# A fused two-layer attention and expert kernel on one core: zeros on TensorE first, value weights and first context tiles in halves

## The reference

```python
x = x + xattn0(layernorm(x), ctx, ctx)      # 64 heads of 8 channels, linear attention:
#   qh = softmax(q over a head's 8 channels); kh = softmax(k over the 512 channels of a row)
#   kvs = kh^T v per head;  out = qh kvs
x = x + ffn0(layernorm(x), U1, V1, U2, V2, b1, b2)
x = x + xattn1(layernorm(x), ctx, Wq, Wk, Wv, Wo)   # k, v = [ctx, layernorm(x)] @ Wk.T, Wv.T
x = x + experts(layernorm(x), ...)                  # top 4 of 16 experts, and a shared one
```

## Time and profile before

| what | value |
|---|---|
| median of 3 runs | 724.55 us (724.33 to 725.87) |
| the profiled execution's own time | 721.26 us |
| its span, first to last instruction | 719.2 us |
| PE busy | 681.9 us, 95% of the span |
| DVE / ACT / POOL busy | 47% / 28% / 24% |
| mean granted PE clock | 0.99 |

### The profile page before, as it was taken

The page is one execution under the profiler, slowest core; times in us unless marked ns, Lnnn a source line. Parts: engine busy times, 40 slices in busy tenths (PEclk is TensorE's granted clock), DMA queues, the critical chain, the costliest instruction groups (busy, mean ns, idle before and its releaser), DMA issues.

```text
span 719.2 us, 9656 instructions
## 1 busy us (share of the span) xinstructions
PE 681.9 (95%) x2428; PEld 392.0 (55%) x2429; DVE 341.2 (47%) x831; ACT 200.6 (28%) x562; POOL 175.9 (24%) x226
## 2 busy tenths in 40 slices
PE   5999999999999999999999999999898999999991
PEld 3555344446777777767776665544343444444440
DVE  3898332532223546576675767555132333223330
ACT  4453332323335433333323342231111111111110
POOL 2344310101000000040404324264032322232332
PEclk9999999999999999999999999999999999999997
DMA  9999996004000020010104102028878757866544
GB/s 328 410 420 420 422 422 284 0 6 170 1 0 1 1 88 0 1 59 1 59 1 147 58 1 118 1 88 190 300 180 193 180 102 179 216 140 105 93 61 56
DMA packets 54481, 98.97 MB, mean 138 GB/s; under 512 B 6528, under 2 KB 27776, under 8 KB 53792
## 3 DMA queue, kind: packets, MB, share of 16 engines
q1 hardware_dynamic: 24704, 69.02, 26.0%
q0 software_dynamic: 8816, 18.00, 12.6%
q10 hardware_dynamic: 20928, 11.54, 5.6%
HBM read 44.50 MB, written 54.17 MB: 137 GB/s over the span
## 4 chain that ended last, share of the span: by engine, by line
PE 78%; DMA 10%; DVE 4%; issue 2%; ACT 1%; SPq 1%; ACTq 1%; POOL 1%; POOLq 1%; DVEq 0%
PE ps L1110 44%; PE ps L1271 11%; DMA out<-rq,sidx 8%; PE ps L1240 4%; PE ps L1101 4%; PE ps L1256 4%; PE ps L1189 3%; PE ps L1190 3%; PE ps L1199 2%; DVE rq L910 2%; DMA rq<-in_Wv 1%; PE ps L1209 1%; DMA kv<-in_experts 1%; PE ps L1133 1%; PE ps L1134 1%
## 5 line engine op out<-in xcount | busy, mean ns | idle before, releaser
L1110 PE MATMUL ps<-kv,rq 128*128 x432 | 194.8, 599 | 4.8 <-SPq L482 3.7
L1110 PEld LDWEIGHTS ps<-kv,rq 128*128 128x128 f32 x432 | 79.4, 191 | 93.7 <-issue 93.2
L1110 PE MATMUL ps<-zT,r 128*128 128x256 f32 (+1 forms) x424 | 103.4, 400 | 0.9 <-ACT kv L654 0.9
L1110 PEld LDWEIGHTS ps<-zT,r 128*128 128x128 f32 x424 | 79.5, 190 | 20.2 <-issue 10.2
L582 POOL DMA_INDIRECT out<-rq,sidx x36 | 56.6, 1573 | 116.6 <-DMA out<-rq,sidx 85.2
L1271 PE MATMUL ps<-r 128*128 128x512 f32 x192 | 85.1, 593 | 0.0
L513 POOL TENSOR_SCALAR ve<-mv 128x1 f32<-128x1 f32 x32 | 7.1, 222 | 301.9 <-DVE mv L879 301.9
L692 ACT ACTIVATE r<-ps,snm 128x128 f32<-128x128 f32 x128 | 45.2, 365 | 82.4 <-DVE snm L966 82.4
L1050 DVE TENSOR_TENSOR rq<-ps,rq 128x256 f32<-128x256 f32 x36 | 15.3, 424 | 100.1 <-ACT rq L745 100.1
L1271 PEld LDWEIGHTS ps<-r 128*128 128x128 f32 x192 | 35.2, 190 | 38.3 <-issue 38.3
L745 ACT ACTIVATE rq<-ps 128x256 f32<-128x256 f32 x36 | 13.8, 383 | 128.3 <-PE ps L1110 113.7
(11 more groups left out here) (163 smaller groups left out, 864.4 us busy)
## 6 DMA issues: line engine op xcount, KB each, us to landing
slot_rows<-rq SPq DMA_DIRECT2D x4, 8192.0 KB, 49.0
kv<-in_experts SPq DMA_DIRECT2D x54, 256.0 KB, 5.2
rq<-slot_rows ACTq DMA_DIRECT2D x136, 64.0 KB, 2.8
r<-in_Wq SPq DMA_DIRECT2D x1, 3072.0 KB, 21.1
r<-in_Wo SPq DMA_DIRECT2D x2, 1536.0 KB, 8.3
r<-in_ctx SPq DMA_DIRECT2D x8, 256.0 KB, 8.9
xr<-in_x SPq DMA_DIRECT2D x8, 256.0 KB, 8.7
out<-xr SPq DMA_DIRECT2D x8, 256.0 KB, 2.9
```

What stands on the lines that cost most here:

```text
L1110: mm = pe.matmul(out, lhs(k), rhs(k), start=(k == 0), stop=(k == n - 1))
```

## The change

Four things are changed.

1. PE no longer begins with a wait for `cst`. It waits for two memsets and multiplies a 128x128 tile of zeros 12 times (`WARM`) into a bank of PSUM that is not yet used. The wait for `cst` now stands at the first transpose.
2. `wv` and the first `ctxT` quarter are loaded in halves of the contraction (k = 0, 1 and k = 2, 3). The second half of `wv` goes to SP's queue, as its third DMA.
3. A new step `kv_half` makes the first halves of units v0 and v1, before the first transposes. Their second halves stand where units stand.
4. The opening order changes: the shift of tile 0 stands ahead of `a_stat 1`, `a_q 0` stands behind two units, and three units stand in the opening where there were two. In return pass j = 1 of the loop has one unit and not two.

```diff
+WARM = 12
...
-        prog += [("a_stat", 0), ("a_stat", 1), ("a_prep", 0), ("a_t", 0), ("a_q", 0), ("a_prep", 1), unit(), ("a_stat", 2),
-                 ("a_kvs", 0), ("a_t", 1), ("a_prep", 2), ("a_q", 1), unit(), ("a_stat", 3)]
+        prog += [("a_stat", 0), ("a_prep", 0), ("a_stat", 1), ("kv_half",), ("a_t", 0), unit(), ("a_prep", 1), unit(),
+                 ("a_q", 0), ("a_stat", 2), ("a_kvs", 0), ("a_t", 1), ("a_prep", 2), unit(), ("a_q", 1), ("a_stat", 3)]
...
-            if j in (1, 3, 5, 6):
+            if j in (3, 5, 6):
                 prog.append(unit())
...
             sp.dma_start(cst[:, 0:2 * P], cst_d[:, 0:2 * P]).then_inc(s_cst, 16)
+            sp.dma_start(wv[:, 2:4, :], wv_d.rearrange("p (k m) -> p k m", k=KC)[:, 2:4, :]).then_inc(s_wv[1], 16)
...
-            for h in range(2):
-                act.dma_start(ctxT[:, :, h * 256:(h + 1) * 256], ctxT_d[:, :, h * 256:(h + 1) * 256]).then_inc(s_ct[h], 16)
-                if h == 0:
-                    act.dma_start(wv, wv_d.rearrange("p (k m) -> p k m", k=KC)).then_inc(s_wv, 16)
+            act.dma_start(ctxT[:, 0:2, 0:256], ctxT_d[:, 0:2, 0:256]).then_inc(s_ct0[0], 16)
+            act.dma_start(wv[:, 0:2, :], wv_d.rearrange("p (k m) -> p k m", k=KC)[:, 0:2, :]).then_inc(s_wv[0], 16)
+            act.dma_start(ctxT[:, 2:4, 0:256], ctxT_d[:, 2:4, 0:256]).then_inc(s_ct0[1], 16)
+            act.dma_start(ctxT[:, :, 256:512], ctxT_d[:, :, 256:512]).then_inc(s_ct[1], 16)
...
-            pe.wait_ge(s_cst, 16)
+            pe.wait_ge(s_ms, 2)
+            for i in range(WARM):
+                pe.matmul(ps[:, 3, 0:P], zero[:, :], zero[:, :], start=True, stop=True)
...
+            def half_unit(j, i):
+                for k in (2 * i, 2 * i + 1):
+                    mm = pe.matmul(kv_bank(j)[:, 0:G * HD], ctxT[:, k, j * P:(j + 1) * P], wv[:, k, :],
+                                   start=(k == 0), stop=(k == KC - 1))
+                return mm
...
+                if kind == "kv_half":
+                    pe.wait_ge(s_ct0[0], 16)
+                    pe.wait_ge(s_wv[0], 16)
+                    for j in range(2):
+                        half_unit(j, 0)
+                elif kind == "a_t":
+                    j = step[1]
+                    if j == 0:
+                        pe.wait_ge(s_cst, 16)
```

More of the change, by code:

```diff
@@ L169, in build @@
         s_wk = sem("wk_loaded")
-        s_wv = sem("wv_loaded")
+        s_wv = [sem(f"wv_loaded{i}") for i in range(2)]
+        s_ct0 = [sem(f"first_ctxT_loaded{i}") for i in range(2)]
         s_ct = [sem(f"ctxT_loaded{h}") for h in range(J // 2)]
@@ L1089, in _, with context_loaded @@
         def _(pe):
-            pe.wait_ge(s_cst, 16)
+            pe.wait_ge(s_ms, 2)
+            for i in range(WARM):
+                pe.matmul(ps[:, 3, 0:P], zero[:, :], zero[:, :], start=True, stop=True)
+            def context_loaded(j):
+                if j < 2:
+                    for i in range(2):
+                        pe.wait_ge(s_ct0[i], 16)
+                else:
+                    pe.wait_ge(s_ct[j // 2], 16)
             def tbank(step):
@@ L1111, in dense @@
                 return mm
+            def half_unit(j, i):
[3 more added lines that the diff above has]
+                return mm
             for step in prog:
                 kind = step[0]
-                if kind == "a_t":
+                if kind == "kv_half":
[4 more added lines that the diff above has]
+                elif kind == "a_t":
                     j = step[1]
+                    if j == 0:
+                        pe.wait_ge(s_cst, 16)
                     pe.wait_ge(s_ek, j + 1)
@@ L1121, in _ @@
                     pe.wait_ge(s_trc, TRN[("a_t", j)] + 1)
-                    pe.wait_ge(s_ct[j // 2], 16)
+                    context_loaded(j)
                     if j >= 2:
@@ L1158, in _ @@
                               lambda k: src[:, k, h * 512:(h + 1) * 512], KC).then_inc(s_pr, 1)
+                    elif n < 2:
+                        pe.wait_ge(s_wv[1], 16)
+                        half_unit(unit[1], 1).then_inc(s_pr, 1)
                     else:
-                        pe.wait_ge(s_wv, 16)
                         j = unit[1]
```

## The result

The changed kernel takes 718.19 us in the median of four runs (717.69 to 719.22), before 724.44 us of four (723.53 to 725.87). The ratio is 0.9926, with a 95% interval from 0.9905 to 0.9946: faster by 0.7%. The forecast was faster, but 722.1 us, and its range ended at 720.5. The profiled executions stand at 717.69 and 721.26 us.

A forecast was written before the change was run, and what follows sets the result against it. The prediction took PE and the x3 load to limit the opening, then DVE. Gaining 0.4 us at the first reciprocal, 2.5 us in all by the third, it put 724.55 - 2.5 = 722.1 us, range 720.5 to 724.0.

The forecast's parts named there:

- the third path: Opening: the load of x3 keeps landing at 18.05, so DVE's first long reciprocal starts no sooner than 19.09.
- R0: Start of DVE's long reciprocal for tile 0; forecast to go from 19.47 to 19.1, a gain of 0.4 us.
- their failure: Opening: the zeros leave PE's clock low; up to 1.65 us longer, 1.4 covered, loss about 0.3; no chance of its own.
- PE's path: Opening: PE's work through v2, ending at 16.3, allows the first long reciprocal at about 18.5.
- the wait for ek 1: Opening: transposes 1 wait for ek 1 at 13.2 while PE is free at 12.6, covering 0.6 us of clock loss.
- The moved unit: v3 moved from pass 1 into the opening; DVE's third long reciprocal at 32.6 against 35.15, a gain of 2.5 us.
- R2: Start of DVE's long reciprocal for tile 2; forecast at 32.6 with no idle time of DVE ahead of it.
- PE's whole 4.15 us: Opening: PE's idle 2.50 us for `wv` plus 1.65 us of low clock in v0.
- The larger gain: Rival: all of PE's 4.15 us come off, 720.4 or less; needs x3 about 1 us earlier; chance 0.08.
- x0 did not land late: Rival on SP's queue: x0 lands after 10.5, at 11.68 at the latest, leaving a gain of 0.8; chance 0.17.
- The halves landed late: Rival in the opening: first halves land no sooner than `wv` did, at 9.3; gain 0.8, 723.8 us; chance 0.12.
- The rule against the halves: Loads: 2.0 us fixed cost per DMA would land x0 2.0 us later, the gain falling to about 1.0 us.

The follow-up runs named there:

- e1: The kernel before, unchanged, timed and profiled again as a control; ratio to before 1.0003.
- e7: The changed kernel with the second half of `wv` on ACT's queue and not SP's; ratio to before 0.9955.
- e9: The changed kernel, unchanged, timed and profiled a third time; ratio to before 0.9923.
- e10: The kernel before, unchanged, timed and profiled a third time; ratio to before 0.9989.
- e3: The changed kernel without the 12 multiplications of zeros (`WARM = 0`); ratio to before 0.9976.
- e14: The changed kernel, unchanged, profiled once more for the spread of its opening; sixth `a_out` at 52.15 us.
- e16: The changed kernel, unchanged, profiled once more for the spread of its opening; sixth `a_out` at 52.03 us.
- e5: The kernel before with only the third unit moved into the opening and out of pass 1; ratio to before 1.0003.
- e4: The changed kernel with the third unit put back into pass 1; zeros, halves and loads stay; ratio to before 0.9967.
- e2: The changed kernel, unchanged, timed and profiled a second time; ratio to before 0.9951.
- e11: The changed kernel with the whole loads of before and no `kv_half`; zeros and moved unit stay; ratio to before 0.9977.
- e6: The kernel before with only the split loads of the change; no zeros, order and whole units of before; ratio to before 1.0010.
- e13: The kernel before, unchanged, profiled once more for the spread of its opening; sixth `a_out` at 56.28 us.

## Why the prediction was wrong

**The step that failed** is the third path of "What DVE makes of it": "so I keep 18.05 and with it R0 no sooner than 19.09". Tile 3's loads do limit R0, but not there. In the changed kernel x3 landed at 6.22 + 10.7 = 16.9, and in the other four profiles of it at 16.8 to 17.4. The prediction's own sign of being wrong, x3 moving by more than half a microsecond, came. Nor was 18.05 a constant of before: in e1 the same load landed at 5.81 + 11.1 = 16.9, and in the five profiles of before anywhere from 16.9 to 18.1. I took one execution's landing for a property of the kernel. R0 came at 17.8 to 17.9 in four of five profiles, 1.2 us before the forecast's 19.1.

What sets R0 in these four is a tie. From the start of DVE's maximum of tile 3 it is 1.6 us to R0 (16.27 to 17.88), and that tile's context rows landed at 16.1 to 16.3, so the loads allow R0 no sooner than 17.7 to 17.9. In e7, with x0 there 1.7 us earlier, DVE waited for the same rows and could not have begun R0 before 17.8. DVE's own row of small steps allows about the same: in e9, where it waits for no load behind x0, it takes 9.2 us from x0's landing (8.58) to R0 (17.80). The prediction had 9.1 for it (18.5 less 9.47 is 9.03), partly by luck: it counted 2.0 us from `kvm 0` to R0 for PE and left out DVE's own 2.6 (15.21 to 17.80 in e9), while the steps ahead were shorter than it had them. In the first profile x0 was there sooner, at 8.22, and R0 was not; DVE waited 0.30 us for x2.

**A second size was off.** The sum was made against a profile with a good opening: R0 at 19.47 where the median of five is 19.86. The lower clock cost v0 1.65 us there and up to 2.7 (5.26 less 2.59) in e10. So the change saves 0.4 more against a usual run. 2.5 + 1.2 + 0.4 = 4.1, against 4.16 between medians. That takes 724.4 to 720.3, just past the range's end at 720.5.

**The zeros were sized too low.** The prediction gave their failure about 0.3 us, since it put the loads' limit 0.6 us behind PE's path. With the loads 1.2 us sooner PE's path decides when the zeros are left out, and e3 loses 1.5 us; the wait for ek 1, which was to cover part of it, was gone too.

**What held.** The zeros ended at 5.8, `kv_half` started at 5.79 (6.1 forecast; 6.3 in e9, e14 and e16) with 0.33 us for a piece. The moved unit pays 2.18 us, by the step that the prediction gave (34.3 us from R0 to the sixth `a_out`: 53.4 less 19.1), and it pays through DVE's 2.07 us ahead of R2. e5 and e4 show both halves of that. PE's whole 4.15 us was not what came off, and that the sum comes so near it is luck: the 4.16 between medians is 1.98 at R0 and 2.18 later. R0 waited for no PE instruction, R2 had no idle time ahead of it, and the stretch from there to the tables kept its length. PE's extra idle time ahead of `a_out 1` was forecast at 1 to 2 us and was 0.18 (0.90 less 0.72).

**The rivals.** The larger gain, 720.4 or less at a chance of 0.08, is the only case on record whose time takes in the measured 718.2, and the condition that it named, x3 about 1 us sooner, came true; its mechanism, all of PE's idle time and clock loss coming off, did not. The stated range ended 0.1 us short of that rival's own time. x0 did not land late: 8.13 to 8.83, though more stood ahead of it on its queue. The halves landed late once, in e2, and then by 2 us and with the clock's fall on top. The rule against the halves did not show either. It was worked out from the fixed cost of about 2.0 us for each DMA that the Trainium skill, DMA: Bandwidth & Descriptors, "Anatomy of one DMA — SWDGE (gpsimd) path", has for transfers issued from GpSimd. By it x0 in the change, with one transfer more ahead of it, would land 2.0 us later; it landed at 8.13 to 8.83, before at 8.34 to 9.47.

**What stays open.** Why the first landings differ by 1 to 2 us from run to run is not settled, nor whether the change itself moves x3: with the loads of before it landed at 16.6 in e5 and 16.8 in e11 too. The first timing gained 6.2 us between medians, e2 4.3 and e9 5.0. The 4.16 us of the opening lie inside all three intervals, but no profile shows where the other 2.1 us of the first timing come from; that the late stretch takes part in it is not shown.

## What to carry to other kernels

When two engines alternate, time won on one of them pays in full only where the other waits for it. Look for such a wait further on and move work out of that place into the time won: here the moved unit showed no gain alone (e5), the time won alone 1.3 us in one profile (e4), and both together 4.2. Take a landing time or a clock loss from several profiles before it is made a hard limit, above all at the start of a kernel. Starting TensorE on idle work was worth 1.5 us here (e3), and not in every execution: with 1.30 us of idle time ahead of the real work the clock held (e11), with 2.01 us it fell (e2).

## What the runs showed that was not expected

- After the zeros, an idle stretch of 1.30 us left v0 at the upper level (e11); one of 2.01 us was followed by the lower level (e2: granted clock 0.55 from 8.7 to 12.0). In e4 2.18 us of idle time later on was followed by a granted clock of 0.69 from 15 to 20 us.
- In five of the profiles (e1, e6, e9, e13, e16) the granted clock reads 0.93 between 140 and 165 us, and the stretch from the sixth `a_out` to the tables is 436.5 to 436.8 us and not 435.1. It hit both kernels.
- The stretch behind the tables differs by up to 7 us between executions (226.4 to 233.7). Part of it is one wait of PE ahead of the last shared down products: 0.24 us in before, 2.90 in the change, 6.50 in e3.
